# A 3x3 convolution on TensorE fed from unbroken lines, with GpSimd copying the side taps' operands

## What is computed

```python
x = x + _L1_conv_ref(_ln_c(x), ...)          # _ln_c: normalise over the channels
# inside, with N, H, W, C = 16, 16, 16, 256 and 128 features out:
y = conv_general_dilated(x, entry_w, (1, 1), 'SAME', ...)   # 3x3, zero border
y = relu(y * entry_s + entry_b)
qv, qh, feat = (relu(y @ w * s + b) for each of three 1x1 convolutions)
# attention down the columns, a channel gate, attention along the rows, a gate, a 1x1 convolution
```

## Time and profile before

| | us |
|---|---|
| median of 3 runs | 1138.05 (1137.79 to 1139.34) |
| profiled execution, first to last instruction (its span) | 1136.6 |
| TensorE busy | 995.8 (88%) |
| VectorE busy | 615.9 (54%) |
| ScalarE busy | 530.4 (47%) |
| GpSimd busy | 267.8 (24%) |
| mean granted TensorE clock | 0.887 |

### The profile page before, as it was taken

One profiled execution on the slowest core, in us unless ns is written; L12 is line 12 of the kernel. 1 busy time (PEld: TensorE's weight loads), 2 busy tenths in 40 slices (PEclk: granted clock), 3 DMA queues, 4 the chain that ended last, 5 costly groups with the idle time before them and its releaser, 6 DMA issues. The chain is left out here.

```text
span 1136.6 us, 19741 instructions
## 1 busy us (share of the span) xinstructions
PE 995.8 (88%) x5614; PEld 807.2 (71%) x5614; DVE 615.9 (54%) x1713; ACT 530.4 (47%) x1344; POOL 267.8 (24%) x274
## 2 busy tenths in 40 slices
PE   6866579999999999993688999999884799998999
PEld 1743368888888888882466666776543699997998
DVE  6887643332332232224756577555778455554776
ACT  6536444443444444433243443433324466666774
POOL 0000021111111111104752200000000344442776
PEclk9558659999999999996789999999655599999999
DMA  9544411111111111205532201101140244443554
GB/s 382 237 149 148 149 32 52 52 52 56 52 52 56 55 52 53 57 29 172 182 120 84 66 28 57 38 19 75 65 139 19 92 139 141 136 137 117 171 182 144
DMA packets 63235, 114.68 MB, mean 101 GB/s; under 512 B 9698, under 2 KB 43124, under 8 KB 62132
## 3 DMA queue, kind: packets, MB, share of 16 engines
q1 hardware_dynamic: 49908, 77.72, 19.3%
q0 software_dynamic: 12960, 35.41, 11.0%
q10 hardware_dynamic: 288, 0.47, 0.1%
HBM read 73.96 MB, written 39.59 MB: 100 GB/s over the span
## 5 line engine op out<-in xcount | busy, mean ns | idle before, releaser
L600 POOL DMA_INDIRECT experts_rows_sb<-h_rows,choices x142 | 134.3, 946 | 731.3 <-POOLq L428 401.8
L795 DVE TENSOR_TENSOR experts_a_sb<-experts_a_sb,experts_bankU 128x512 f32<-128x512 f32 x71 | 48.9, 689 | 225.3 <-PE experts_bankU L183 225.3
L746 ACT ACTIVATE experts_a_sb<-experts_bankG 128x512 f32<-128x512 f32 (+1 forms) x142 | 69.7, 491 | 92.7 <-PE experts_bankG L183 92.6
L737 ACT ACTIVATE experts_hT<-experts_bankH 128x256 fp32r<-128x256 f32 x142 | 54.3, 382 | 90.5 <-PE experts_bankH L663 90.2
L759 ACT ACTIVATE experts_y_sb<-experts_bankY 128x256 f32<-128x256 f32 x142 | 54.7, 385 | 87.6 <-PE experts_bankY L180 66.8
L1182 POOL DMA_INDIRECT attn_y<-y_rows,choices x64 | 65.7, 1027 | 92.4 <-POOLq L120 38.1
L181 PE MATMUL attn_bankC<-attn_padded,attn_w_high 128*128 128x512 f32 x144 | 68.0, 472 | 16.7 <-ACT attn_feat L1468 14.0
L916 POOL DMA_INDIRECT shared_y<-y_rows,choices x64 | 67.5, 1055 | 38.5 <-POOLq L555 19.3
L180 PE MATMUL experts_bankY<-down_plain,experts_aT_plain 128*128 x284 | 72.9, 379 | 0.0
L186 DVE TENSOR_TENSOR experts_aT<-experts_bankA,experts_aT 128x256 fp32r<-128x256 f32 x142 | 59.7, 420 | 23.0 <-ACT experts_aT L754 23.0
L670 PE MATMUL experts_bankA<-konst_sb,experts_a_sb 128*128 128x128 f32 x426 | 70.0, 273 | 1.7 <-DVE experts_aT L186 1.7
(11 more groups left out here) (370 smaller groups left out, 2752.7 us busy)
## 6 DMA issues: line engine op xcount, KB each, us to landing
y_rows<-experts_y_sb SPq DMA_DIRECT2D x142, 128.0 KB, 1.7
h_rows<-xn SPq DMA_DIRECT2D x32, 256.0 KB, 2.1
mix_xT<-in_xt SPq DMA_DIRECT2D x4, 1024.0 KB, 12.3
x_res<-in_x SPq DMA_DIRECT2D x4, 1024.0 KB, 14.1
gate_raw<-in_L_ffn_gate_w SPq DMA_DIRECT2D x2, 2048.0 KB, 13.0
up_raw<-in_L_ffn_up_w SPq DMA_DIRECT2D x1, 4096.0 KB, 24.9
x_rows<-x_res SPq DMA_DIRECT2D x16, 256.0 KB
x_res<-x_rows SPq DMA_DIRECT2D x8, 512.0 KB, 4.8
```

Source lines behind the costliest of these rows:

```text
L600: nc.gpsimd.indirect_dma_start(rows[t % DEPTH][:, :], None, h_dram, bass.IndirectOffsetOnAxis(ap=ids_i[:, t:t + 1], axis=0)).then_inc(s_ro ...
L746: nc.scalar.activation(a_sb[i % RING][:, :], bankG[i % RING][:, 0:hidden], ACT.Silu if gate is not None else ACT.Relu).then_inc(s["act"], 1)
L795: nc.vector.tensor_tensor(a_sb[i % RING][:, :], a_sb[i % RING][:, :], bankU[i % RING][:, 0:hidden], ALU.mult).then_inc(s["a"], 1)
```

## The change

`padded` loses its border columns and the borders between images: the two images of a pair are interleaved line by line, a line of both is 32 elements, and a zero line stands before each block, with one more behind the last. For the middle taps (dc = 1) the moving operand is then one unbroken run of 512 elements. For the left and right taps there are new tiles `beside[0]` and `beside[2]`, high and low, of one pair each, in which every line is moved by one column with a zero column at the edge. GpSimd fills them with two copies for each side (`shift`), after `lows` of both images, and, from the second pair on, after the previous convolution has left that tile (`conv_left` for the left side, `conv` for the right). TensorE takes the taps in the order middle, left, right, and waits for `shifted0` at step 6 and `shifted2` at step 12. The ring `y_in` shrinks from 16 to 8 buffers. GpSimd's order is now: gathers of pairs 0 and 1, shifts of pair 0, gathers of pair 2, shifts of pair 1, and so on. The Relu reads bankC with the interleaved order. VectorE clears other borders (16 memsets for 8). Three small bias tiles move into the space of `branches`.

```diff
...
 PT = 2 * HALVES
 BATCH = IMAGES // 2
 GATE = 5
-W2 = COLS + 2
-IMG = (ROWS + 2) * W2
+LINE = 2 * COLS
+PAD = (ROWS + 1) * LINE
+SIDES = (0, 2)
 STEPS = 9 * KC
-Y_RING = 4 * PT
+Y_RING = 2 * PT
 AXES = ("down", "along")
-s = {n: sem(f"attn_{n}") for n in ("border", "w_high", "w_low", "mask", "tables", "sum", "chain", "var", "log", "root", "rstd", "xn", "turned", "high", "lows", "conv",
+s = {n: sem(f"attn_{n}") for n in ("side_border", "conv_left", "shifted0", "shifted2", "border", "w_high", "w_low", "mask", "tables", "sum", "chain", "var", "log", "root", "rstd", "xn", "turned", "high", "lows", "conv",
...
 s_x = [sem(f"attn_x{p}") for p in range(PAIRS)]
 with ExitStack() as early:
     y_in = [sb(f"attn_y{g}", [P, C], on=early, side="right") for g in range(Y_RING)]
-    padded = [sb(f"attn_padded{n}", [P, RING * KC * 2 * IMG], HALF, on=early, side="right") for n in range(2)]
+    padded = [sb(f"attn_padded{n}", [P, RING * KC * PAD + LINE], HALF, on=early, side="right") for n in range(2)]
+    beside = {dc: [sb(f"attn_beside{dc}_{n}", [P, KC * PAD + LINE], HALF, on=early, side="right") for n in range(2)] for dc in SIDES}
     w_high = sb("attn_w_high", [P, STEPS * F], HALF, on=early, side="right")
     with ExitStack() as raw:
         w_raw = sb("attn_w_raw", [P, STEPS * F], on=raw, side="right")
...
 gates = sb("attn_gates", [F, 64], on=on)
 mask = {ax: [sb(f"attn_mask_{ax}_{side}", [9, P], HALF, on=on) for side in "lr"] for ax in AXES}
 table = {"down": "same_col", "along": "same_row"}
-bias_raw = sb("attn_bias_raw", [2, 3 * F], on=on)
-bias_part = [sb(f"attn_bias_part{n}", [2, 3 * F], HALF, on=on) for n in range(2)]
 bias_rows = sb("attn_bias_rows", [2, 3 * F], HALF, on=on)
 ones2 = sb("attn_ones2", [2, P], HALF, on=on)
 branch_sb = sb("attn_branch", [BATCH, F], on=on)
 branches = sb("attn_branches", [P, IMAGES * F], on=on)
+bias_raw = branches[0:2, 0:3 * F]
+bias_part = [branches[0:2, (n + 1) * 3 * F:(n + 2) * 3 * F].bitcast(HALF) for n in range(2)]
 bankC, bankT, bankQ, bankF, bankX, bankG = (pb(f"attn_bank{n}", 512, on=on) for n in "CTQFXG")
 bankS = {ax: pb(f"attn_bankS_{ax}", 512, on=on) for ax in AXES}
 bankP = {"down": bankQ, "along": bankF}
...

 def image(part, kc, n):

-    at = (n // 2 % RING * KC + kc) * 2 * IMG + n % 2 * IMG
-    return padded[part][:, at:at + IMG].rearrange("p (y z) -> p y z", z=W2)[:, 1:ROWS + 1, 1:COLS + 1]
+    at = (n // 2 % RING * KC + kc) * PAD
+    return padded[part][:, at:at + PAD].rearrange("p (y n z) -> p y n z", n=2, z=COLS)[:, 1:ROWS + 1, n % 2, :]

 def turned(kc):
     return bankT[:, kc * 256:(kc + 1) * 256].rearrange("p (y z) -> p y z", z=COLS)
...
     sp.dma_start(w_raw[:, :], A["conv_w"]).then_inc(loads["conv"], 16)
     sp.wait_ge(s["sum"], PT)
     load_x(1)
-    sp.dma_start(bias_raw[:, :], A["out_rows"][:, 3 * F:6 * F].broadcast_to([2, 3 * F])).then_inc(loads["attn"], 16)
+    sp.dma_start(bias_raw, A["out_rows"][:, 3 * F:6 * F].broadcast_to([2, 3 * F])).then_inc(loads["attn"], 16)
     load_attention(sp)
     rows = h_dram.rearrange("(j p) c -> p j c", p=P)
     loaded = 0
...

 @block.gpsimd
 def _(pool):
-    for p in range(PAIRS):
+
+    def gather(p):
+        if not has(p):
+            return
         for k, t in order(p):
             u, j = place(p, k, t), p * PT + t
             if u >= Y_RING:
...
             nc.gpsimd.indirect_dma_start(
                 y_in[u % Y_RING][:, :], None, y_dram,
                 bass.IndirectOffsetOnAxis(ap=pos_i[:, j + k * TILES:j + k * TILES + 1], axis=0)).then_inc(s_in[u % Y_RING], 16)
+
+    def shift(p, dc):
+
+        pool.wait_ge(s["lows"], p * 2 + 2)
+        if p:
+            pool.wait_ge(s["conv_left" if dc == 0 else "conv"], p)
+        to, of = (1, 0) if dc == 0 else (0, 1)
+        for part in range(2):
+            lines = [x.rearrange("p (k y z) -> p k y z", k=KC, z=COLS)[:, :, 2:2 * ROWS + 2] for x in (
+                beside[dc][part][:, 0:KC * PAD], padded[part][:, p % RING * KC * PAD:(p % RING + 1) * KC * PAD])]
+            last = nc.gpsimd.tensor_copy(lines[0][:, :, :, to:to + COLS - 1], lines[1][:, :, :, of:of + COLS - 1])
+        last.then_inc(s[f"shifted{dc}"], 1)
+
+    gather(0)
+    gather(1)
+    pool.wait_ge(s["side_border"], 1)
+    for p in range(PAIRS):
+        if p:
+            gather(p + 1)
+        for dc in SIDES:
+            shift(p, dc)

 @block.tensor
 def _(pe):
...
             if p:
                 pe.wait_ge(s["feat"], p)
         for step in range(first, end):
-            kc, dr, dc = step // 9, step % 9 // 3, step % 3
-            base = (p % RING * KC + kc) * 2 * IMG
-            pair = [x[:, base:base + 2 * IMG].rearrange("p (n y z) -> p n y z", n=2, z=W2)
-                    [:, :, dr:dr + ROWS, dc:dc + COLS] for x in padded]
+            dc, kc, dr = (1, 0, 2)[step // (3 * KC)], step // 3 % KC, step % 3
+            if dc == 1:
+                base = (p % RING * KC + kc) * PAD + dr * LINE
+                pair = [x[:, base:base + ROWS * LINE] for x in padded]
+            else:
+                if step % (3 * KC) == 0:
+                    pe.wait_ge(s[f"shifted{dc}"], p + 1)
+                base = kc * PAD + dr * LINE
+                pair = [x[:, base:base + ROWS * LINE] for x in beside[dc]]
             at = ((dr * 3 + dc) * KC + kc) * F
             last = product(bankC[:, :], [x[:, at:at + F] for x in w_half], pair, step == 0, step == STEPS - 1)
+            if step == 2 * 3 * KC - 1:
+                last.then_inc(s["conv_left"], 1)
         if end == STEPS:
             last.then_inc(s["conv"], 1)

...
             act.wait_ge(s["projected"], p)
         for n in range(2):
             part = slice(n * 256, (n + 1) * 256)
-            last = nc.scalar.activation(feat[:, part].rearrange("p (h y z) -> p h y z", h=2, y=ROWS), by_column(bankC[:, part]), ACT.Relu,
+            of = bankC[:, :].rearrange("p (y n h z) -> p n h y z", y=ROWS, n=2, h=2)[:, n]
+            last = nc.scalar.activation(feat[:, part].rearrange("p (h y z) -> p h y z", h=2, y=ROWS), of, ACT.Relu,
                                         bias=entry_sb[:, 1:2], scale=entry_sb[:, 0:1])
         last.then_inc(s["feat"], 1)

...
             nc.vector.scalar_tensor_tensor(out=il_w[:, kc * F:(kc + 1) * F], in0=il_w[:, kc * F:(kc + 1) * F], scalar=1.0 / (ROWS * COLS),
                                            in1=scales_b[:, F:2 * F], op0=ALU.mult, op1=ALU.mult)
         nc.vector.tensor_copy(ones2[:, :], K("ones", 2))
-        chain(nc.vector.tensor_copy(bias_part[0][:, :], bias_raw[:, :]))
-        chain(low_half(nc.vector, bias_part[1][:, :], bias_raw[:, :], bias_part[0][:, :]))
-        chain(nc.vector.tensor_scalar(bias_raw[:, :], bias_part[0][:, :].bitcast(F32), K("ident", 2)[:, 0:1], None, ALU.mult))
-        nc.vector.scalar_tensor_tensor(out=bias_rows[:, :], in0=bias_part[1][:, :].bitcast(F32), scalar=K("ident", 2)[:, 1:2], in1=bias_raw[:, :],
+        chain(nc.vector.tensor_copy(bias_part[0], bias_raw))
+        chain(low_half(nc.vector, bias_part[1], bias_raw, bias_part[0]))
+        chain(nc.vector.tensor_scalar(bias_raw, bias_part[0].bitcast(F32), K("ident", 2)[:, 0:1], None, ALU.mult))
+        nc.vector.scalar_tensor_tensor(out=bias_rows[:, :], in0=bias_part[1].bitcast(F32), scalar=K("ident", 2)[:, 1:2], in1=bias_raw,
                                        op0=ALU.mult, op1=ALU.add).then_inc(s["tables"], 1)

     def low_weights(n):
...

     for gate in ("rows", "cols"):
         nc.vector.memset(sums[gate][:, :], 0.0)
+    def zero_lines(x, blocks):
+
+        lines = x[:, 0:blocks * PAD].bitcast(F32).rearrange("p (n i) -> p n i", i=PAD)
+        nc.vector.memset(lines[:, :, 0:LINE], 0.0)
+        return nc.vector.memset(x[:, blocks * PAD:blocks * PAD + LINE].bitcast(F32), 0.0)
+
     for part in range(2):
-        images = padded[part][:, :].bitcast(F32).rearrange("p (n i) -> p n i", i=IMG)
-        nc.vector.memset(images[:, :, 0:W2], 0.0)
-        nc.vector.memset(images[:, :, IMG - W2:IMG], 0.0)
-        by_row = images.rearrange("p n (y z) -> p n y z", z=W2)
-        nc.vector.memset(by_row[:, :, 1:ROWS + 1, 0:1], 0.0)
-        last = nc.vector.memset(by_row[:, :, 1:ROWS + 1, W2 - 1:W2], 0.0)
+        last = zero_lines(padded[part], RING * KC)
     last.then_inc(s["border"], 1)
+    for dc in SIDES:
+        for part in range(2):
+            zero_lines(beside[dc][part], KC)
+            edge = beside[dc][part][:, 0:KC * PAD].bitcast(F32).rearrange("p (k y z) -> p k y z", k=KC, z=COLS)
+            at = 0 if dc == 0 else COLS - 1
+            last = nc.vector.memset(edge[:, :, 2:2 * ROWS + 2, at:at + 1], 0.0)
+    last.then_inc(s["side_border"], 1)
     for k in range(2):
         add_routed(0, k, FIRST)
     statistics(0, FIRST)
```

## The result

| | before | changed |
|---|---|---|
| median of 5 runs, us | 1137.79 (1135.37 to 1139.34) | 1162.76 (1159.48 to 1165.02) |
| profiled execution, span, us | 1136.6 | 1160.6 |
| first convolution matmul of pair 0 to that of pair 7, us | 205.8 | 234.8 |

The change makes the kernel slower by 25 us: the ratio is 1.0226, with a 95% interval of 1.0205 to 1.0247. The profiled execution of the changed kernel took 1162.76 us, 2.2 more than its span. All of it is lost in one stretch: from the stage's first VectorE instruction to the last convolution matmul it took 257.9 us before and takes 287.5 now, 29.6 more. Outside that stretch these two profiles differ by 5.6 us the other way, in stages of the same code: 2.1 ahead of it and 3.5 behind it.

What follows compares the result with a forecast made beforehand. TensorE was taken as the bound late and not early, VectorE as nearly a second; the start's delay, late gathers and faster matmuls gave -1.7 us, contention +7.2, so +5.5 on 1138.05: 1143.5 us, range 1132 to 1164.

Steps and rivals of the forecast that it cites:

- rival 4: Slow GpSimd copies of 1.9 us, rows later still, VectorE held up to 3.4 us: 1152 to 1164 us; chance 0.28.
- The gain: Convolution matmuls on TensorE: 11 us at most for eight pairs, only partly collected where VectorE and ScalarE end last.
- The pitch: Spacing of convolution matmul starts on TensorE: from 0.260 to 0.233 us with contiguous operands, 0.027 us less each.
- The price of a copy: GpSimd: four copies a pair of 960 elements per partition, 1.1 us each, 4.4 us a pair.
- Rival 3: The matmuls win: copies of 0.85 us, `deviations` not held, about -4 to -5 us, 1133.5; chance 0.22.
- Late gathers: Gathers queued behind GpSimd's copies: rows summed 4.8 us late at the start, 3.3 in iteration 4, partly absorbed by VectorE's waits.
- The sum without contention: Whole kernel: start's delay, late gathers and TensorE's gain together, with no engine held by another, -1.7 us.
- the ring of 8: Gathered-row buffers: waiting on eight is no bound, as pair p+1 was summed an iteration before.
- The forecast of waits for rows in iterations 0 to 5: VectorE would wait for DMA ahead of L1596 in iterations 0 to 5, where there were hardly any waits.
- Contention: Copies hold VectorE's `deviations` ahead of the Relu: 1.2 us (bounds 0 and 1.8) at six convolution starts, 7.2 us.
- the start's 3.1 us: Start of the stage: pair 2's gathers come late behind pair 0's copies, so convolution 1 starts some 3.1 us later.
- The clock: TensorE, an aside in rival 4: iterations ending in waits of 2 to 8 us have mean clocks 0.77 and 0.92.

Runs made afterwards that it cites:

- run 4: Changed kernel without GpSimd's copies, all taps reading the unbroken middle lines, so the sums are not the reference's: 1131.82 us, ratio 0.9953 to the kernel before.
- run 8: Changed kernel with each GpSimd copy replaced by a zero fill of the same 960 elements, reading nothing, so sums are wrong: 1139.80 us, ratio 1.0020 to the kernel before.
- run 5: Kernel before the change with 8 buffers for gathered rows instead of 16, nothing else: 1137.76 us, ratio 0.9996 to the kernel before.
- Run 9: Changed kernel with unread filler matmuls in TensorE's wait for the Relu ahead of convolutions 1 to 6: 1154.87 us, ratio 1.0164 to the kernel before.
- run 6: Changed kernel with each GpSimd copy of 960 elements split into two of 480: 1149.97 us, ratio 1.0124 to the kernel before.
- run 3: Changed kernel with pair p+2's gathers ahead of pair p's copies, and copies after the next pair's `deviations`, both from pair 1 on: 1144.81 us, ratio 1.0062.
- run 7: Changed kernel with the copies moved from GpSimd to ScalarE, behind the Relu and the feat2 copy: 1129.51 us, ratio 0.9926 to the kernel before.

## Why the prediction was right and wrong

The forecast was 1143.5 us, 5.5 over the kernel before; measured are 1162.76, 25 over it. Slower was right, and so was its mechanism, copies that hold VectorE's small instructions ahead of the Relu. What failed is the step that priced it: 1.2 us at each of six starts, 7.2 in all, where the runs give some 23, and the half clock behind the longer waits, which the sum had at nothing. That the measured time still lies in the range of 1132 to 1164 is luck: rival 4 had stretched it that far for another reason.

**The gain.** The pitch was right: 0.23 us. That part of it would only lengthen TensorE's wait was right too; in place of 11 us run 4 has 6.

**The price of a copy.** It was taken at 1.1 us from VectorE's row of 1024 elements and is 0.95 (four in 3.78 us beside the small instructions alone, 4.11 where the pair of 256 elements runs too). Rival 4, whose range holds the measured time, gave the loss to copies of 1.9 us and is wrong in its cause, though it also had longer holds and the half clock. Rival 3 asked for copies near 0.85 us and an unheld `deviations`: not so.

**Late gathers.** The sum without contention was -1.7 us; run 8, which has the lateness without the reading, measured +2.6 us by its medians, with 0.7 us of hold left in it. Pair 0 grew by 4.0 us (3.1 taken), and pairs 1 to 7 gave back 2.0 us in all, where 4.8 had been credited. The gathers' lateness did mostly fit into VectorE's waits, as reckoned for iterations 1 to 5, but it used up TensorE's gain as well. (Iteration 1 was read too small: its last sum ended 8.7 us behind `lows`, so 9.2 us late and not 1.6; a wait of 7.64 us behind it took most of that.) That the ring of 8 is no bound was right (run 5). The forecast of waits for rows in iterations 0 to 5 failed in the changed kernel: past iteration 2 the hold slowed all so much that the gathers were in time.

**Contention: the step that failed.** The mechanism was named with its place, and `deviations` is where it struck, though the row that was taken to show the lock is a thin one: of the other gather issues in that trace that overlapped three or four sums, three took 0.94 to 1.09 us and one 2.07. Its upper bound was 2c less the slack, 1.8 us, and 1.2 was taken. The bound assumed that only the two copies of one side could meet the chain, and that a few small instructions share one wait. Neither holds: both sides' copies run back to back (only pair 2's leave 0.65 us between the sides), since convolution p-1 ends before the first two are done, and VectorE gets one instruction in between two copies. The chain has four gaps for four copies, and loses 1.5 to 3.0 us (0.95 before, 2.5 to 4.0 now); with the two instructions of L1762, which the prediction left out though they too have two SBUF inputs and stand ahead of the chain, it is 3.1. The Relu wait grew by 3.2 us at convolutions 4 to 6, not 1.2. In iteration 0 the four sums also met the copies and lost 3 us, which the start's 3.1 us didn't contain; convolution 1 started 7.6 us later into the stage. Run 8 against the changed kernel gives the term its size, clock included: 23 us where 7.2 stood.

**The clock.** It stood in rival 4 as an aside and in the sum with nothing. Run 9 gives back 7 to 8 us by its medians and 11 in its profile by filling the waits alone. So part of the 23 us is half clock, by these medians about a third, but its size stays open. In convolutions 4 to 6 it comes with the growth of the Relu wait from 0.4 to 3.6 us. Rival 4 tied the clock of a stretch to the wait at its end; the half clock lies behind the wait at its start: in the kernel before, pair 3's stretch began behind a wait of 2.27 us, ended with one of 0.40, and had a clock of 0.94. By the Trainium skill (TensorE: Matmul & The Clock Gate, HAM oscillation) idle gaps between bursts of matmuls make the clock fall; the trace agrees, with 0.43 us a matmul behind the 3.62 us wait, where 0.23 stood ahead of it.

The account of the 25 us, from the medians (in brackets from the ratios): -6.0 (-5.3) for unbroken lines, +8.6 (+7.6) for GpSimd's being busy and the gathers late, +22.4 (+23.4) for its reading, with the half clock that follows from each. By the Trainium skill (SBUF — State Buffer, Who interferes with whom) a GpSimd instruction that only writes SBUF doesn't meet one with two SBUF inputs, and a VectorE one in a two-port mode, which tensor_scalar can be in, meets both kinds. The changed kernel's trace and runs 6 and 8 agree: 0.16 us under a fill, 0.92 under a copy of 960, 0.50 under one of 480, and the one-input L1660 held by the fill too. Whether L1660 ran in such a mode no row shows.

## What to carry to other kernels

Work put on an idle engine isn't free by that: look what its neighbour does at that moment. A chain of tiny VectorE instructions beside back-to-back GpSimd copies lost one copy for each instruction that met one, up to four here, and not one in all. Price it by the number of instructions or of copies, whichever is smaller, and put the copies where a row shows a wait of that length on an engine whose work the copies don't slow (ScalarE's here, of which 2.68 us were left behind four copies). And where two delays lie side by side, undoing one alone shows little; what TensorE then waits can be paid again, in part, at half clock.

## What the runs showed of the hardware that I had not expected

- A held VectorE instruction of four elements takes nearly as long as a GpSimd copy: 0.89 to 0.97 us beside copies of 960 elements (four in 3.78), 0.48 to 0.51 beside those of 480 (eight in 4.30), against 0.16 free.
- A GpSimd fill, which reads nothing, leaves two-input instructions alone and still holds a one-input one of 128x4 (0.86 us against 0.17).
- Behind the waits of 3.6 us the granted clock was half for 6.8 to 10.2 us, longer than the wait; behind the 0.56 us wait at convolution 4 in runs 3, 4 and 7 it stayed full.
- A GpSimd copy of 960 fp32 elements per partition takes 0.95 us, nearly as long as ScalarE's (0.92: 3.68 us for four).
